# An attention and expert-layer kernel on one core: squares on ScalarE, key sums on GpSimd, preparation in tiles of its own from slot 0, four led groups of maxima

## What is computed

```python
x = x + attn(layernorm(x), W_attn, W_proj)      # x: (4, 1024, 128), 16 heads of 8
x = x + ffn(layernorm(x), ...)

# attn: keys and values are sums over aligned blocks of 4, 8, ..., 1024 tokens, and a tail
k_cum, v_cum = cumsum(k), cumsum(v)
K, V = slices of k_cum, v_cum over the blocks    # a token sees the blocks that ended before it
logits = concat([q @ K.T * scale (masked), sum(q * K_tail) * scale])
att = softmax(logits); out = att[..., :-1] @ V + att[..., -1:] * V_tail

# ffn: 32 experts of 64 (6 chosen out of 4 of 8 groups), and a shared one of 256
scores = sigmoid(x @ gate_w.T); ...top-k...; combine = (T, 32) weights
h = relu(x @ up_w.T)**2 * combine ; moe = h @ down_w
shared = relu(x @ shared_up_w.T)**2 @ shared_down_w.T
```

## Time and profile before

| what | value |
|---|---|
| median of 3 runs | 822.89 us (816.61 to 824.41) |
| the profiled execution | 823.96 us |
| its span, first to last instruction | 822.0 us |
| busy: PE, DVE, ACT, POOL | 655.7, 493.3, 310.8, 281.2 us |
| one expert layer of the loop | 139.85 to 251.25 us, 111.4 us |
| one attention of the loop | 258.5 to 341.16 us, 82.7 us |

### The profile page before, as it was taken

One profiled execution on the slowest core, in us unless ns is written; L12 is line 12 of the kernel. 1 busy time (PEld: TensorE's weight loads), 2 busy tenths in 40 slices (PEclk: granted clock), 3 DMA queues, 4 the chain that ended last, 5 costly groups with the idle time before them and its releaser, 6 DMA issues.

```text
span 822.0 us, 13199 instructions
## 1 busy us (share of the span) xinstructions
PE 655.7 (80%) x3986; PEld 313.6 (38%) x3986; DVE 493.3 (60%) x1146; ACT 310.8 (38%) x435; POOL 281.2 (34%) x385
## 2 busy tenths in 40 slices
PE   4368777979887887887988788788798887888897
PEld 1223322534543232353553233244445332325453
DVE  3647872577644787267744587536783569825832
ACT  2215347324122445632422334652242162482232
POOL 2301212444651112155364111125546312025575
PEclk9669999999899999999989999999998999999999
DMA  6330000000420000000042000000014300000000
GB/s 191 110 66 4 2 1 2 27 0 1 134 53 16 3 2 1 2 26 0 20 116 52 17 2 2 2 27 1 0 41 104 55 4 2 1 1 1 1 13 13
DMA packets 19624, 22.98 MB, mean 28 GB/s; under 512 B 4105, under 2 KB 17609, under 8 KB 18281
## 3 DMA queue, kind: packets, MB, share of 16 engines
q1 hardware_dynamic: 19560, 22.17, 10.4%
HBM read 14.95 MB, written 6.82 MB: 26 GB/s over the span
## 4 chain that ended last, share of the span: by engine, by line
issue 29%; PE 29%; DVE 25%; POOL 8%; ACT 4%; DMA 2%; SPq 1%; DVEq 1%; POOLq 0%; ACTq 0%
DVE MXR L1171 8%; PE om L1009 5%; PE om L1074 5%; POOL PT L714 4%; PE ring L915 4%; PE ring L1055 3%; ACT PT L788 3%; DVE XN L1124 2%; DVE PT L1324 2%; PE om L902 2%; PE ring L993 1%; PE ring L956 1%; PE ring L988 1%; DVE stats L1113 1%; PE ring L1063 1%
## 5 line engine op out<-in xcount | busy, mean ns | idle before, releaser
L714 POOL TENSOR_TENSOR PT<-PT 128x512 f32<-128x512 f32 x144 | 185.4, 1295 | 239.4 <-DVE PT L1324 171.0
L1171 DVE TENSOR_REDUCE MXR<-ring 128x4 f32<-128x1024 f32 (+2 forms) x192 | 178.1, 952 | 76.5 <-PE ring L956 71.0
L788 ACT ACTIVATE PT<-ring 128x1024 f32<-128x1024 f32 x160 | 156.6, 1024 | 145.4 <-PE ring L993 145.1
L816 ACT ACTIVATE PT<-ring 128x512 f32<-128x512 f32 x144 | 86.0, 597 | 187.0 <-PE ring L1055 185.9
L1074 PE MATMUL om<-PT,wdown 128*128 128x512 f32 x288 | 148.8, 598 | 0.0
L1324 DVE TENSOR_TENSOR PT<-PT,ring 128x512 f32<-128x512 f32 x128 | 86.3, 684 | 76.8 <-ACT PT L816 64.2
L1009 PE MATMUL om<-PT,VA 128*32 128x512 f32 (+1 forms) x768 | 89.5, 553 | 26.2 <-ACT PT L788 26.2
L1055 PE MATMUL ring<-XH,WUH 128*128 128x512 f32 x144 | 98.3, 683 | 0.0
L915 PE MATMUL ring<-dense 128*128 128x512 bf16 x226 | 72.8, 413 | 22.6 <-DVE MXR L1171 16.0
L1063 PE MATMUL ring<-CT,exp_sel 96*128 96x512 bf16 x128 | 51.9, 405 | 32.9 <-DVE PT L1324 32.9
L630 POOL TENSOR_TENSOR MS<-MALL,zeros 128x16 bf16<-128x16 f32 x32 | 7.3, 230 | 180.6 <-DVE MALL L1186 172.8
(11 more groups left out here) (141 smaller groups left out, 814.6 us busy)
## 6 DMA issues: line engine op xcount, KB each, us to landing
QA<-q_parts SPq DMA_DIRECT2D x96, 64.0 KB
q_parts<-Qparts SPq DMA_DIRECT2D x24, 128.0 KB
KA<-k_parts SPq DMA_DIRECT2D x48, 64.0 KB
X<-in_x_dram SPq DMA_DIRECT2D x4, 512.0 KB, 3.8
out_dram<-Y SPq DMA_DIRECT2D x8, 256.0 KB, 3.0
k_parts<-Kparts SPq DMA_DIRECT2D x12, 128.0 KB
PT<-in_up_dram SPq DMA_DIRECT2D x1, 1152.0 KB, 5.8
QA<-MB SPq DMA_DIRECT2D x64, 6.0 KB
```

Source lines behind the costliest of these rows:

```text
L714: pool.tensor_tensor(H[:, u % 4, :], src[:, u % 4, :], R[:, u % 4, :], ALU.mult).then_inc(s_h, 1)
L788: act.activation(dst, src, ACT.Exp, scale=SCALE).then_inc(s_exped, 1)
L816: act.activation(R[:, u % 4, :], st[:, u % 2, :], ACT.Relu).then_inc(s_relu, 1)
L1171: ins = dve.reduce_max(MXR[:, g, i, :, q0:q0 + nq], banks(("max", u))[:, :, at:at + ns * nq].rearrange("p e (q s) -> p e q s", s=ns), AX.X)
```

## The change

- **Squares.** ScalarE takes relu into R and then, after a wait for that relu, Square of R: for routed units into V, for shared units straight into H. VectorE multiplies V by the broadcast weights into H. GpSimd has no part in it any more. In a slot, VectorE's product of unit v-1 now stands ahead of the slot's steps; it stood behind them.
- **GpSimd** does `tails` and `sums` of the keys too (in the loop; VectorE still does them in the prologue), and `norm` of window 1, of which VectorE did the two large products.
- **Own tiles.** The preparation has XP, XNP, norm1 and its own transposed tile, where it shared X, XN, stats and XNT with the steps behind the attention. X of the next batch is loaded twice, into XP at the start of a body and into X behind the preparation's DMAs.
- **Tables.** `PREP_AT` spreads the preparation over slots 0 to 26 (it was 15 to 29), with long steps cut in two; the two fillers in each of its slots are gone. `POST_AT` has some steps cut in two and ends at slot 18 instead of 16.
- **Led maxima.** All four groups of window 0 are led (12 units and 3 `mT`), from slot 27 to 38; there were 6 units and one `mT` in slots 34 to 39. In the prologue too. `ORDER` has 72 ring units instead of 78 and is laid anew.

```diff
-PREP_AT = {15: ["ln_stats"], 17: ["ln_apply0"], 18: ["ln_apply1"], 19: ["f0", "f1"], 20: ["f4", "f5"], 21: ["tails_k", "f2"],
...
+PREP_AT = {0: ["ln_stats0"], 1: ["ln_stats1"], 2: ["ln_stats2"], 5: ["ln_apply0"], 7: ["ln_apply1", "f0"], 9: ["f1"], 10: ["f4"],
+           11: ["f5"], 12: ["f2", "tails_k", "sums_k"], 13: ["f3"], 14: ["f6"], 15: ["f7"], 18: ["ksplit0"], 19: ["ksplit1"],
+           20: ["qsplit00", "tails_v"], 21: ["qsplit01", "sums_v"], 22: ["qsplit10"], 23: ["qsplit11", "f9"], 24: ["prod", "f10"],
+           26: ["f11", "f8"]}
...
-LEAD_GROUPS = 2
+LEAD_GROUPS, LEAD_ROWS = 4, 3
...
-LEAD_FROM = 34
+LEAD_FROM, LEAD_SLOTS = 27, 12
...
+                elif step == "tails_k" and not first:
+                    chaink.begin(p - 1)
+                    pool.wait_ge(s_pevac, p * FILLS + max(done_after("f4"), done_after("f5")))
+                    tails(pool, chaink, 0)
+                elif step == "sums_k" and not first:
+                    sums(pool, chaink, 0)
...
-                    pool.tensor_tensor(H[:, u % 4, :], src[:, u % 4, :], R[:, u % 4, :], ALU.mult).then_inc(s_h, 1)
...
                     act.wait_ge(s_up, b * UNITS + u + 1)
-                    if u >= 4:
-                        act.wait_ge(s_h, b * UNITS + u - 3)
                     act.activation(R[:, u % 4, :], st[:, u % 2, :], ACT.Relu).then_inc(s_relu, 1)
+                    act.wait_ge(s_relu, b * UNITS + u + 1)
+                    if CHUNKS[u % NCH] < 16:
+
+                        if u >= 4 and behind(u):
+                            act.wait_ge(s_h, b * 32 + behind(u))
+                        act.activation(V[:, u % 4, :], R[:, u % 4, :], ACT.Square).then_inc(s_sq, 1)
+                    else:
+                        if u >= 4:
+                            act.wait_ge(s_dn, b * UNITS + u - 3)
+                        act.activation(H[:, u % 4, :], R[:, u % 4, :], ACT.Square).then_inc(s_hs, 1)
...
-                        if v in PREP_AT and not last:
-                            filler(st[:, v % 2, :], 2)
...
-                                pe.wait_ge(s_vw, b * 32 + routed - 1)
+                                pe.wait_ge(s_h, b * 32 + routed - 1)
...
+                    u = v - 1
+                    if 0 <= u < UNITS and CHUNKS[u % NCH] < 16:
+                        dve.wait_ge(s_sq, b * 32 + routed + 1)
+                        dve.wait_ge(s_bc, b * 32 + routed + 1)
+                        if u >= 4:
+                            dve.wait_ge(s_dn, b * UNITS + u - 3)
+                        dve.tensor_tensor(H[:, u % 4, :], V[:, u % 4, :], st[:, 2 + routed % 2, :], ALU.mult).then_inc(s_h, 1)
+                        routed += 1
```

More of the change, by code:

```diff
@@ L165, in attention_order @@
     steps = [(w, g, k) for w in range(NW) for g in range(NG) for k in range(len(PV_STEPS[w]))]
-    rows = [(w, g) for w in range(NW) for g in range(NG)][1:]
+    rows = [(w, g) for w in range(NW) for g in range(NG)][LEAD_ROWS:]
     turns, post = [], list(POST_STEPS)
@@ L169, in attention_order @@
         done["mfin", 0, g] = 0.0
-    done["rows", 0, 0] = 0.0
+    for g in range(LEAD_ROWS):
+        done["rows", 0, g] = 0.6 + 0.8 * g
+    if LEAD_GROUPS == NG:
+        order.append(("tail", 0, 0, 0))
     ring = lambda: done[RING[-3]] if len(RING) >= 3 else 0.0
@@ L282, in misc_order @@
 def misc_order():
-    uses = [("mT", 0, 0), ("yT", 1, 0)]
+    uses = [("mT", 0, g) for g in range(LEAD_ROWS)] + [("yT", 1, 0)]
     for kind, w, g, n in ORDER:
@@ L668, in post_step @@
             def post_step(b, w, step):
-                if step == "norm" and w == 0:
+                if step == "norm":
                     heads, flat = by_head(w)
-                    chain2.begin(b)
+                    chain2.begin(NW * b + w)
                     freed(pool, b, ("oT", w, NG - 1))
@@ L800, in attend, with behind @@
                         post_step(b, w, n)
+            def behind(u):
+                return sum(CHUNKS[m % NCH] < 16 for m in range(u - 3))
             def down_evac(b, w):
@@ L1132, in prep_step @@
                 elif step in ("ln_apply0", "ln_apply1"):
                     t0 = WT * int(step[-1])
-                    ln_apply(X, range(t0, t0 + WT), s_rstd1, p + 1, s_xn1)
-                elif step == "tails_k":
+                    ln_apply(XNP, XP, norm1, range(t0, t0 + WT), s_rstd1, p + 1, s_xn1)
+                elif step == "tails_k" and first:
+                    chaink.begin(0)
                     dve.wait_ge(s_pevac, p * FILLS + max(done_after("f4"), done_after("f5")))
-                    tails(dve, chain1, 0)
-                elif step == "sums_k":
-                    sums(dve, chain1, 0)
-                elif step == "ksplit":
+                    tails(dve, chaink, 0)
+                elif step == "sums_k" and first:
+                    sums(dve, chaink, 0)
+                    chaink.end()
+                    dve.sem_inc(s_sumk, 1)
+                elif step == "ksplit0":
+                    dve.wait_ge(s_sumk, p + 1)
```

182 lines of the change are left out of this document (90 added, 92 removed).

## The result

The changed kernel takes **779.49 us** (median of 4 runs, 769.91 to 786.21) against 823.65 us for the kernel before on the same chip: a ratio of 0.945, 95% interval 0.932 to 0.959. A second measurement gave 773.06 us and 0.934 (0.925 to 0.943). The ratios leave out the executions of either kernel that ran some 2% longer than its fastest in a slower state. The forecast of 753 us had the right sign and was 20 to 26 us too low; the measured time lies inside the range of 732 to 788. The profiled execution, the fastest of the four, took 769.91 us with a span of 768.1, where the span before was 822.0: 53.9 us went, not 69.9. So 16 of the missing us are to be found in the trace; the rest lies between this execution and the median.

What follows compares the result with a forecast made beforehand. TensorE's own work was taken as the floor of each stage, with VectorE, held by GpSimd, making it wait. Terms 11.1 - 28 - 46.5 - 6.5 = -69.9 on a span of 822.0 gave 753 us, range 732 to 788.

Steps and rivals of the forecast that it cites:

- Squares: Expert layers: moving 36 products from GpSimd to ScalarE gives back VectorE's stalls, 7 us per looped batch, about three in the last.
- rival (e): Expert layers: ScalarE paces the units at 2.3 instead of 1.25 us each; no change, 823 us; chance 0.02.
- VectorE in the expert layer: Looped expert layer: VectorE work from 68.85 to some 63 us, losing 1 to 2 us before cT in slot 18.
- TensorE in the expert layer: Looped expert layer: 91 us of TensorE work plus idle time, sum 96; -15.5 per layer, bounds -8 and -20.
- Led units and the DMA: First led unit in slot 27: slots cover the query rows' 13.8 us, with an estimated 2 us to spare.
- The prologue term: Prologue: two further led groups, at 5.54 us per group, are covered by nothing and cost +11.1 us.
- Attention: Attention stages: 6 of 78 ring units go; -7 us each, -28 for four, bounds -3 and -12.
- Last expert layer: Last expert layer: TensorE idles 8.2 us, of which two for norm stay; -6.5 us, bounds -3 and -8.
- (a): Slots 11 to 18: GpSimd's sums hold VectorE by the lock; layer saves 8 instead of 15.5, 776 us; chance 0.2.
- (b): Looped layers: each led unit costs 1.85 us as in the prologue instead of hiding; +23, 776 us; chance 0.1.
- (c): Attention: it closes its gap, -12 instead of -7 us in each, 733 us; chance 0.13.
- (d): Expert layers: without fillers TensorE's clock falls to 1.2 GHz; one whole layer so, about 840 us; chance 0.03.

## Why the prediction was right in sign and wrong in size

**Squares: right in sign, and the reason holds only in part.** VectorE's stalls and the broadcast's waits went as said; alone the edit gave 8.5 per looped layer and 7.15 in the last, where 7 us of VectorE and "about three" stalls stood. The stalls were 11 and 3, of 5.9 and 2.5 us, so in the last layer most of the gain came some other way (the product's new place or the shorter chain; not separated). Relu, wait and square come to 1.34 us per unit (188.98 to 190.32) against the 1.25 taken; the square starts 0.1 us after the relu's end, inside the bounds. Square's length was 0.63 us, not 0.60. ScalarE did not pace the units, so rival (e) falls.

**VectorE in the expert layer: right.** The key sums on GpSimd are worth 16 us in slots 0 to 26 of three layers. On VectorE they took 4.7 us where 5.4 were taken. Slot 17, where cT waits, is 2.68 us longer than a plain one (4.47 less 1.79), and slots 18 and 19 give back 0.8 of it (1.24 and 1.55 against 1.79); 1 to 2 were forecast.

**TensorE in the expert layer: undersized gain.** With the rows in time the first looped layer would be some 92 us, an estimate (99.81 less the 7.7 of slots 27 to 29), where the forecast said 96. I had the changed kernel at 91 us of work and 5 of waits, and the work is 87.6, with a slow clock in part of it. My own terms, 91 and 5.5 to 6, made 96.5 to 97, not 96, so the -15.5 was 0.6 to 1.1 too much by its own sum.

**Led units and the DMA: this step failed.** The prediction priced the journey of the query rows by one row, 13.8 us in the prologue, and gave it "an estimated 2 us to spare; if not, the cost is a few us times three". It takes 19.86 us in batch 0 where 13.8 were priced, the cover is 14.1 where some 16 were counted on, and the journey varies: from the store to the second loads 15.5 to 26.5 us over the batches of all fourteen traces. The cost is some 20 us in the loop (late led units and the half clock that follows) and 3.0 in the prologue. That is more than the 16 us by which the sum missed; the larger gains in the attention and in the layers' own work make the difference. The kernel before held the warning: in its own loop the journey to the second loads took 17.13 us at 139 GB/s, then 20.61 and 22.02 in the two batches after, where the prologue's took 15.48, and it showed this in a place where nothing waited. The prologue term itself, +11.1, measured +11.8. That the time is inside the range is owed to the upper end, which allowed for a cover that fails three times, though not for some 20 us.

**Attention: right.** -5.4 in the first, and 75.84 us in place of 82.66 in the second; with the loop's edge and the end of the layer it came to -32.1 against -28. The term itself was 7 for two more groups (its six units at 1.06 us are 6.4, not 6.2). Between the kernels that differ in that (and in slots) the stretch from slot 35 to the next slot 0 shrinks by 3.9 us (97.73 to 93.87, cT in slot 19) or by 8.0 (99.75 to 91.69, cT in 18). Why these differ stays open.

**Last expert layer: -4.6 against -6.5.** The squares alone gave -7.15. What is missing from the forecast is cT (1.6, shown by moving it), which it priced only in the looped layers. The wait for `norm` is as forecast, 2.25 us where two were left; it was 2.23 before and 1.52 with the squares alone, so it is a part of what the change has less than the squares alone.

**The rivals.** (a) falls by the run with the key sums on VectorE. (b) is half right: a led unit is not serial at 1.85 us but costs 2.5 us per group of three units and its transposed row, where the term had 1.75; leading the third and fourth groups doesn't pay for itself anywhere. (c) did not happen as a whole: the attention gave 4 us more than forecast, not 20. Of (d) a little did, by a way that it didn't name: the clock fell after idle time at the led units, in slots 27 to 29, and not for want of fillers elsewhere. The 776 us of (a) or (b) lie beside the measured 773 and 779, and that is luck.

Four led groups are thus the one part of the change that is shown to have lost time. Without them, and with cT one slot on, the rest is worth 10 to 11% instead of 5.5 to 6.6.

## What to carry to other kernels

Price a round trip through DRAM by the slowest instance that the trace has, and look for it where nothing waits for it too: the DMA share and the GB/s of its window tell whether it is a delay or a transfer that runs at its rate. Work that is led into an earlier stage costs there what it takes from TensorE; it pays only as far as it fills an idle start, here with the second group, and the way to find that is to count one group more and one less. When a wait is put on TensorE, add what the clock takes afterwards; here that was 1.4 to 2.7 us per batch.

## What the hardware showed that was not expected

The same 30 transfers with the same bytes took between 15.5 and 26.5 us, in one program and even in one execution (16.38, 23.32 and 16.77 us in consecutive batches), at a DMA share that stayed near a half. The loads' packets of 8 KB made the difference, with 0.335 to 0.792 us on average, while the stores' packets of 1 KB kept to about 0.05. A load that was cut into 1-KB packets took twice as long to issue, 0.69 against 0.34 us, and made the journey slower but steady, 24.8 to 26.2 us. After a wait of 5.75 us TensorE ran at half its clock, and the slot after it took 3.78 us in place of 2.38; after a wait of only 0.49 us that slot took 4.01.
